# Two deformable convolutions: low halves to VectorE, tents and padded copies to ScalarE, images written out

## The reference

```python
x = x + deformable_conv(_ln_c(x))     # offsets from a 3x3 convolution, batch norm and relu
t = t + lstm_like(_ln_t(t))           # 256 steps, one after the other
x = x + deformable_conv(_ln_c(x))     # the second kind, without batch norm
t = t + top2_of_8_experts(_ln_t(t))
```

```python
py, px = base_y + ky - 1 + dy, base_x + kx - 1 + dx
sampled = (v00*(1-fy)*(1-fx) + v01*(1-fy)*fx + v10*fy*(1-fx) + v11*fy*fx) * mod
out = einsum('bckhw,ock->bohw', sampled, w)
```

## Time and profile before

| | us |
|---|---|
| median of 3 runs (1077.59 to 1084.23) | 1082.31 |
| the profiled execution | 1078.73 |
| its span, first to last instruction | 1076.9 |
| busy: TensorE | 802.8 |
| busy: VectorE | 648.6 |
| busy: ScalarE | 592.6 |
| busy: GpSimd | 439.1 |

### The profile page before, as it was taken

How to read it: one execution, slowest core, us unless ns; L and a number is a source line. 1 busy time by engine, 2 the same in 40 slices (tenths; PEclk the granted TensorE clock), 3 DMA queues, 4 the chain that set the end, 5 groups by cost and what they waited for, 6 DMA issues and landing times.

```text
span 1076.9 us, 18938 instructions
## 1 busy us (share of the span) xinstructions
PE 802.8 (75%) x6224; PEld 589.6 (55%) x6224; DVE 648.6 (60%) x1576; ACT 592.6 (55%) x1660; POOL 439.1 (41%) x343
## 2 busy tenths in 40 slices
PE   5687787666666666666666468886867999899996
PEld 3465575555555555555555435665653666556664
DVE  3999992355535445433333358999716776656775
ACT  1566664333335445333333336766646888778884
POOL 0577884000000000000000006878735888768885
PEclk9898988555555555555555568999876999999998
DMA  9500000000001100000000000000000010010000
GB/s 221 132 2 0 0 1 1 1 1 1 0 1 66 72 1 1 1 1 1 1 1 1 1 1 1 2 0 0 0 1 1 2 70 2 14 60 2 2 2 20
DMA packets 5852, 18.41 MB, mean 17 GB/s; under 512 B 1093, under 2 KB 2822, under 8 KB 5254
## 3 DMA queue, kind: packets, MB, share of 16 engines
q1 hardware_dynamic: 5478, 17.21, 5.6%
q10 hardware_dynamic: 288, 0.13, 0.1%
HBM read 9.47 MB, written 0.52 MB: 9 GB/s over the span
## 4 chain that ended last, share of the span: by engine, by line
POOL 35%; PE 20%; issue 19%; DVE 13%; ACT 11%; DVEq 1%; POOLq 1%; DMA 0%; SPq 0%; ACTq 0%
POOL zw L786 19%; POOL hid L750 15%; PE bank L463 9%; DVE bank L1036 6%; PE bank L465 5%; ACT scan_io L688 5%; ACT tcell L692 4%; DVE hr L1042 4%; PE bank L270 1%; PE bank L303 1%; POOL xs L743 1%; PE bank L282 1%; DVE st L875 1%; PE bank L275 1%; POOLq L785 1%
## 5 line engine op out<-in xcount | busy, mean ns | idle before, releaser
L750 POOL TENSOR_TENSOR hid<-smat,shi 128x512 f16<-128x512 f32 x144 | 216.4, 1526 | 556.1 <-ACT smat L594 555.9
L786 POOL TENSOR_TENSOR zw<-hid,zw 128x512 f16<-128x512 f32 x176 | 203.9, 1159 | 50.4 <-ACT zw L719 39.7
L463 PE MATMUL bank<-hr,lv 64*64 64x8 f32 x512 | 96.7, 261 | 158.1 <-DVE hr L1042 158.1
L463 PEld LDWEIGHTS bank<-hr,lv 64*64 64x64 f32 x512 | 72.5, 200 | 204.8 <-DVE hr L1042 204.7
L1141 DVE SCALAR_TENSOR_TENSOR hid<-bank,wsc,st 128x512 f32<-128x512 f32 x176 | 131.8, 750 | 77.0 <-ACT st L723 68.7
L688 ACT ACTIVATE scan_io<-bank 64x16 f32<-64x16 f32 x256 | 49.3, 193 | 210.7 <-PE bank L465 210.5
L1036 DVE TENSOR_TENSOR_SCAN bank<-scan_io 64x32 f32<-64x32 f32 x256 | 57.5, 224 | 162.3 <-ACT scan_io L688 162.2
L875 DVE TENSOR_TENSOR st<-tent,tentx 128x768 f32<-128x768 f32 x96 | 147.0, 1595 | 1.7
L503 PE MATMUL bank<-st,wh 128*128 128x512 f16 x352 | 136.7, 388 | 12.1 <-POOL st L779 5.4
L723 ACT ACTIVATE st<-bank,wsc 128x512 f32<-128x512 f32 x176 | 121.0, 687 | 35.5 <-PE bank L504 18.0
L504 PE MATMUL bank<-st,wl 128*128 128x512 f16 x352 | 136.6, 388 | 0.0
(11 more groups left out here) (149 smaller groups left out, 1275.2 us busy)
## 6 DMA issues: line engine op xcount, KB each, us to landing
w13s<-w SPq DMA_DIRECT2D x8, 704.0 KB, 16.4
w2f<-w SPq DMA_DIRECT2D x4, 384.0 KB, 26.9
w13s<-wh SPq DMA_DIRECT2D x2, 704.0 KB, 3.4
w13s<-wl SPq DMA_DIRECT2D x2, 704.0 KB, 4.6
wh<-w13s SPq DMA_DIRECT2D x2, 704.0 KB, 4.3
wl<-w13s SPq DMA_DIRECT2D x2, 704.0 KB, 5.4
w2f<-w2p SPq DMA_DIRECT2D x2, 384.0 KB, 5.2
w2p<-w2f SPq DMA_DIRECT2D x2, 384.0 KB, 6.2
```

The costliest lines, as they stand in the source:

```text
L463: nc.tensor.matmul(both[:, 0, t, :], lv[:, C:2 * C], prev, start=False, stop=True, skip_group_check=True)
L750: nc.gpsimd.tensor_tensor(slo[:, place(p, g), :, :], smat[:, g % RING, :, :], shi[:, place(p, g), :, :], ALU.subtract).then_inc(s(c + "s_l ...
L786: nc.gpsimd.tensor_tensor(hl[:, u % MR, :], hid[:, u % MR, :], hh[:, u % MR, :], ALU.subtract)\
```

## The change

It touches the two convolutions only.

- GpSimd keeps the residual addition alone. The low half comes from VectorE (`low`), which reads the transposed group from PSUM: scale, less the high half. `smat` and ScalarE's second copy are gone.
- TensorE may write a bank again only when VectorE's `low` of three groups before is done (`s_low`).
- ScalarE makes the tents (`far` is the absolute distance, then relu(1 - far)) and the padded copies.
- VectorE's work is spread over the groups: `low(m, g)` at each g, and between them outer products of this and the next image, `flats`, `distances`, `weighted`, `tap_images`.
- The steps of image m + 1 sit at other groups on TensorE and ScalarE. The loops are written out, and instructions that only counted semaphores up are gone.

```diff
 TensorE
-                    if waits(NG * m + g - RING + 2):
-                        pe.wait_ge(s(c + "tr_copied"), NG * m + g - RING + 2)
+                    if NG * m + g >= RING:
+                        pe.wait_ge(s(c + "s_low"), NG * m + g - RING + 1)
...
+                for m in range(B):
                     for g in range(NG):
+                        if m + 1 < B:
+                            if g < 2:
+                                offsets(m + 1, g)
+                            elif g == 3:
+                                turn_offsets(m + 1)
+                            elif g == 4:
+                                taps(m + 1, 0)
+                            elif g == 8:
+                                taps(m + 1, 1)
+                        if g == LAG + 2 and m > 0 and m % 2 == 0:
+                            turn(m // 2 - 1)
+                        turn_weights(m, g)
                         if g >= LAG:
+                            sums(m, g - LAG)
+                        elif m > 0:
+                            sums(m - 1, NG - LAG + g)
 ScalarE
+                def pads(m):
+                    if m > 1:
+                        act.wait_ge(s(c + "conv_done"), m - 1)
...
+                        nc.scalar.copy(dst[:, 1:1 + H, x0:x0 + W], src).then_inc(s(c + "pads"), 1)
+                def tents(m):
+                    act.wait_ge(s(c + "dist"), m + 1)
+                    nc.scalar.activation(far[:, :, :, :], dist[:, :, :, :], ACT.Abs).then_inc(s(c + "far"), 1)
+                    act.wait_ge(s(c + "far"), m + 1)
...
+                    nc.scalar.activation(tent[m % 2][:, :, :, :], far[:, :, :, :], ACT.Relu, scale=-1.0,
+                                         bias=epsc[:, 2:3]).then_inc(s(c + "tents"), 1)
+                def high(m, g):
+                    act.wait_ge(s(c + "tr_done"), NG * m + g + 1)
+                    if NG * m + g >= SR:
+                        act.wait_ge(s(c + "sz_done"), NG * m + g - SR + 1)
+                    nc.scalar.activation(shi[:, place(m % 2, g), :, :].rearrange("p k n -> p (k n)"),
                                          bank[3 + g % RING][:, :], ACT.Copy, scale=SSCALE)\
+                        .then_inc(s(c + "s_high"), 1)
...
+                            if g == 2:
+                                offsets(m + 1)
+                            elif g == 4:
+                                turned(m + 1)
+                            elif g == 5:
+                                tents(m + 1)
+                            elif g == 6:
+                                taps(m + 1, 0)
...
+                        if g == 7 and m + 2 < B:
+                            pads(m + 2)
+                        high(m, g)
+                    if m + 1 < B:
+                        taps(m + 1, 1)
 GpSimd
-                        gp.wait_ge(s(c + "tr_copied"), 1 + NG * m + g + 1)
-                        nc.gpsimd.tensor_tensor(slo[:, place(p, g), :, :], smat[:, g % RING, :, :],
-                                                shi[:, place(p, g), :, :], ALU.subtract).then_inc(s(c + "s_low"), 1)
 VectorE
+                def low(m, g):
+                    dve.wait_ge(s(c + "s_high"), NG * m + g + 1)
+                    nc.vector.scalar_tensor_tensor(out=slo[:, place(m % 2, g), :, :].rearrange("p k n -> p (k n)"),
+                                                   in0=bank[3 + g % RING][:, :], scalar=SSCALE,
+                                                   in1=shi[:, place(m % 2, g), :, :].rearrange("p k n -> p (k n)"),
+                                                   op0=ALU.mult, op1=ALU.subtract).then_inc(s(c + "s_low"), 1)
...
+                for m in range(B):
+                    for g in range(NG):
+                        low(m, g)
+                        if g == 0:
+                            outer(m, 2)
+                        elif 2 <= g <= 4:
+                            outer(m, g + 1)
+                        if g == 1 and m + 2 < B:
+                            flats(m + 2)
+                        if m + 1 < B:
+                            if g == 4:
+                                distances(m + 1)
+                            elif g == 5:
+                                weighted(m + 1)
+                            elif g == 6:
+                                outer(m + 1, 0)
+                                tap_images(m + 1, 0)
+                            elif g == 8:
+                                outer(m + 1, 1)
+                                tap_images(m + 1, 1)
```

More of the change, by code:

```diff
@@ L105, in build @@
         dist = sb("dist", [P, 2, 2 * TAPS, 16])
-        ndist = sb("ndist", [P, 2, 2 * TAPS, 16])
+        far = sb("far", [P, 2, 2 * TAPS, 16])
         tent = [sb(f"tent{p}", [P, 2, 2 * TAPS, 16]) for p in range(2)]
@@ L172, in place @@
             return (NG * p + g) % SR
-        def waits(v):
-            return not isinstance(v, int) or v > 0
         S = {}
@@ L185, in build @@
         for l in range(2):
-            for n in ("image", "taps", "conv_done", "om_sb", "omt_ps", "omt_sb", "z_ps", "z_act",
-                      "z_dve", "sig", "tent", "st_ready", "tr_done", "tr_copied", "s_low", "sz_done",
-                      "dist", "ndist", "tents", "osb", "out_ps", "out_sb", "res"):
+            for n in ("pads", "flat", "taps", "conv_done", "om_sb", "omt_ps", "omt_sb", "z_ps", "z_act",
+                      "z_dve", "sig", "tent", "st_ready", "tr_done", "s_high", "s_low", "sz_done",
+                      "dist", "far", "tents", "osb", "out_ps", "out_sb", "res"):
                 s(f"c{l}_{n}")
@@ L388, in conv @@
-                offsets(0, 0, 0)
-                offsets(0, 0, 1)
-                pe.wait_ge(s(c + "taps"), 2)
-                taps(0, 0, 0)
-                turn_offsets(0)
-                taps(0, 0, 1)
-                stream(0, 0, first=True)
-                with pe.Fori(0, BQ - 1) as i:
-                    stream(2 * i + 1, 1)
-                    stream(2 * i + 2, 0, ended=i)
-                stream(B - 1, 1, last=True)
+                offsets(0, 0)
+                offsets(0, 1)
+                turn_offsets(0)
@@ L480, in _ @@
             conv(1)
-            norm(3, [("c1_res", 1 + BQ)])
+            norm(3, [("c1_res", BQ)])
             for j in range(8):
@@ L634, in conv @@
-                offsets(0)
-                taps(0, 0, 0)
-                turned(0, 0)
-                taps(0, 0, 1)
-                stream(0, 0)
-                with act.Fori(0, BQ - 1) as i:
-                    stream(2 * i + 1, 1)
-                    stream(2 * i + 2, 0, ended=i)
-                stream(B - 1, 1, last=True)
+                act.wait_ge(s(f"n{2 * l}_xn"), 2)
+                pads(0)
+                pads(1)
+                offsets(0)
+                turned(0)
+                tents(0)
@@ L881, in conv @@
                 dve.wait_ge(s(f"n{2 * l}_xn"), 2)
-                dve.wait_ge(s("zero"), 2)
-                image(0, 0, 0)
+                flats(0)
                 split_taps(l)
-                image(1, 1, 0)
-                def batch(m, p, b4_next):
-                    offsets(m, p)
-                    outer(m, p)
-                    if b4_next is not None:
-                        image(m + 2, p, b4_next)
-                with dve.Fori(0, BQ - 1) as i:
-                    for p in range(2):
-                        batch(2 * i + p, p, i + 1)
@@ L895, in conv @@
-                for p in range(2):
-                    batch(B - 2 + p, p, None)
+                distances(0)
+                weighted(0)
+                outer(0, 0)
+                outer(0, 1)
+                tap_images(0, 0)
+                tap_images(0, 1)
+                flats(1)
+                for m in range(B):
+                    for g in range(NG):
[6 more added lines that the diff above has]
+                            flats(m + 2)
+                        if m + 1 < B:
+                            if g == 4:
[8 more added lines that the diff above has]
+                                tap_images(m + 1, 1)
```

220 lines of the change are left out of this document (92 added, 128 removed).

## The result

The changed kernel takes 1105.71 us (median of 4 runs, 1103.61 to 1106.83); the kernel before takes 1079.95 beside it (median of 4, 1077.59 to 1084.23). The ratio is 1.0232, 95% interval 1.0189 to 1.0274: slower by 25.8 us.

What follows compares the result with a forecast made beforehand. VectorE, busy 98% in the convolutions, was the bound; afterwards work 14.4, waits 4.15 and clock 1.5 give 20.1 us an image. 15.9 + 7 x 20.1 + 14.0 = 170.6 us per convolution, together +22.9: 1103 us, range 1074 to 1120.

Steps and rivals of the forecast that it cites:

- the work of VectorE: VectorE's instructions for one image in the convolutions after the change: 14.4 us, without waits.
- waits A: VectorE idle before low half 5, while ScalarE does far, tent and high half 5: 2.05 us per image.
- B: VectorE waits at group 8, as TensorE's taps, in front of transposes 8, need the low tap images: 1.25 us per image.
- C: VectorE waits before low half 1 of the next image, behind TensorE's transposes, sums and offsets: 0.75 us per image.
- the clock: TensorE's stop of some 5 us per image brings half clock on the work behind it: 1.5 us, bounds 0.8 to 1.7.
- the start-up: From the start of a convolution to its first low half: 15.9 us.
- The period: Time per image in the convolutions, work plus waits plus clock loss: 20.1 us, bounds 18.3 to 21.2.
- The last image: End of each convolution: nine low halves, four outer products, small waits and the unchanged tail: 14.0 us.
- The clock costs nothing: Rival, chance 0.24: TensorE's stop costs no clock in the convolutions; period 18.3 to 18.8 us, kernel 1081 us.
- VectorE stays the bound: Rival, chance 0.13: the waits shrink; with only the one before low half 5, period 16.5 us, kernel 1051 us.
- The clock never comes up: Rival, chance 0.03: TensorE at half clock throughout the convolutions; period 26 us, kernel 1184 us.
- The rule of the Trainium skill: Keep both tent steps on VectorE, not ScalarE: period about 0.85 us shorter, 12 us over both convolutions.

Runs made afterwards that it cites:

- e2: Changed kernel with ScalarE's tents and VectorE's weighted tents moved from group 5 to group 6: 1104.88 us.
- e5: Changed kernel with 64 unused matrix products on TensorE in front of the taps of group 8: 1084.49 us.
- e1: Changed kernel with the first half of the next image's taps and tap images one group earlier: 1070.45 us.
- e8: e3 with the first flat copy on ScalarE and VectorE's second flat moved to the next image: 1026.33 us.
- e3: Changed kernel reordered: taps one group earlier, tents one group later, distances one outer product earlier, outer(m + 1, 1) at group 7: 1025.72 us.
- e7: e3 with 144 GpSimd subtractions added on data nobody uses, one per high half: 1107.11 us.
- e4: Changed kernel with both tent instructions (absolute value and tent) back on VectorE, behind the distances: 1085.61 us.

## Why the prediction was right, point by point

The mechanism held: the work of VectorE, the waits A, B and C and the clock are where they were forecast, with about the sizes forecast. That the total fits to 3 us is in part luck, as two errors cancel (the start-up, and what lies outside the convolutions).

**VectorE's work.** 14.4 us an image were forecast, 14.35 measured (above); where an addition of GpSimd falls on an outer product it is 14.96 (from 90.36 on, 20.95 less waits of 5.99). The low half took 0.69 to its result and 0.60 to the next start, against 0.75 and 0.67 taken: cheaper by 0.6 an image. The flats and the weighted tents took that back, at 0.76 and 0.48 to the next start for 0.65 and 0.37, with the 0.08 of overlap that is lost at each of the four waits.

**Wait A.** Forecast 2.05, measured 2.04 in every image. That it fits to 0.01 is luck: the high half began 0.68 us after the tent where I had 0.57, and my 2.05 held 0.08 of lost overlap that the trace counts as VectorE's work and not as idle time. The other terms are as forecast: `far` starts 0.03 after the distances end (66.54 + 0.75 to 67.32) and takes 0.68. The place "in front of high half 5" that I named is not what counts, as e2 showed: it is a chain out to ScalarE and back with too little of VectorE's own work beside it.

**Waits B and C.** At full clock (e5) they are 1.30 and 0.88 for the forecast 1.25 and 0.75. e1 wrote the tap images earlier and 35 us went, more than wait B alone (14 x 1.3), as the stop and with it the clock changed too. So the mechanism that I called B, taps waiting for tap images in front of transposes 8, is shown.

**The clock.** Taken at 1.5 us an image, bounds 0.8 and 1.7. The changed kernel less e5 is 1105.7 - 1084.5 = 21.2 us over 14 periods, 1.5 each. The average is right, what it is made of only in part. I had 3.4 us at the lower level; in the image shown it is about 5, from 72.85 to 78.0, and costs 2.3 (0.89 on B, 1.41 on low half 0), above my bound of 1.7. Over the fourteen periods the difference to e5 goes from 2.6 down to 0.8. And it lands not on B and C but on B (2.19 for 1.30) and on low half 0 (1.56 for 0.15), behind the offset convolution's first half at 2.48 us. C did not change (0.89 against 0.88). The premise, that a stop of 3 to 4 us is followed by half the clock, is too plain. The stop in front of the slow stretch of the earlier trace rows was 4.28 us, and the same trace has one of 3.83 with the full level right behind it:

```profile
86.28 0.65 PE L336 MATMUL bank<-ident,st 128*128 128x128 f32 x4 [3.83 <-DVE st L875]
```

**The period** was 20.1 in the forecast. Seven of them lie between the first low half of image 0 (36.77) and that of image 7 (181.42): 144.65 / 7 = 20.66. In the second convolution the same two are

```profile
668.11 0.69 DVE L876 SCALAR_TENSOR_TENSOR hid<-bank,shi 128x512 f16<-128x512 f32 x1 [2.73 <-ACT shi L601]
...
809.40 0.68 DVE L876 SCALAR_TENSOR_TENSOR hid<-bank,shi 128x512 f16<-128x512 f32 x1
```

and 141.29 / 7 = 20.18.

**Mis-sized: the start-up.** The term "15.9" measured 36.77 - 17.59 = 19.2 in the first convolution and 668.11 - 649.72 = 18.4 in the second. I had summed taps, offsets, transposes and high half to 3.2 us at full clock. TensorE had stood 5.78 us for the first tap images, from 31.25 on it ran at the lower level, and these steps took 36.77 - 31.25 = 5.5. The first convolution has 0.8 more in front, as ScalarE's padded copies wait for VectorE's small instructions of the batch norm:

```profile
18.55 1.70 ACT L558 COPY pad<-xn 64x256 f32<-64x256 f32 x4 [4.54 <-DVE bnw L962]
```

The last image took 195.15 - 181.42 = 13.7, for 14.0. The first convolution is thus 19.2 + 144.7 + 13.7 = 177.6 against 170.6, the second 18.4 + 141.3 + 13.6 = 173.3. Of the 9.7 us by which both together exceed the forecast, 5.8 are the start-ups' and 4.5 the periods', less 0.6 for the last images.

**Not foreseen: 5.1 us outside the convolutions,** which hid half of that error in the total; there the forecast was lucky. The first matmuls of the norm behind each convolution (L265) take 1.98 us where they took 3.40 and 3.78. It may be that TensorE is no longer held up by GpSimd's nine last subtractions, 12.92 us, in front of them, but that is not shown. From L265 to the end of the span are 281.4 us, 283.7 before; from the first L265 to the second convolution 453.9, 455.4 before. In e8, which has no such subtractions, one of the two rows is back at 3.67, and the stretch behind it takes 283.1. That makes 1.5 and 2.3 us. The remaining 1.2 lie in front of the first convolution and are not the change's: its normalised input comes at 16.90 here and at 18.12 before, and over all eleven traces at 16.5 to 18.3 whatever the edit (18.16 in e1, 16.73 in e3, 18.25 in e7).

**The rivals.** "The clock costs nothing" was forecast at 1081 and is, in effect, e5: 1084.5. "VectorE stays the bound" would have been faster, and is what e3 reaches, by an order that the change doesn't have: 14.8 us a period against the 14.4 + 2.05 that I gave it. "The clock never comes up" found no support, and e3 and e5 run at 1.00 with all 36 transposes of an image. The Trainium skill's sentence on transposes (TensorE: Matmul & The Clock Gate, section Part 4: PE-mode transpose) would have the clock stay down under them. In e3, where transposes fill 23.4 of the 60 us from 40 to 100, the granted clock is 1.00; the profile lists them as MATMUL and doesn't show whether they run in the mode that the sentence is about.

**The rule of the Trainium skill** that spoke against the tents on ScalarE (ScalarE: Activation LUTs, section Rules for kernel authors) was worth 12 us in the prediction and 20 in e4, of which about 8 go with the clock. The rule is right here. Its reason, the speed of one element, which it gives for bf16, is the smaller part: in float32 `tent` takes 0.46 on VectorE and 0.78 on ScalarE, but `far` takes 0.76 and 0.68, 1.22 us against 1.46 together. The larger part is the way to ScalarE and back, 2.04 us of waiting. And in e3, where the chain is covered, ScalarE's tents stand on no one's path.

## What to carry to other kernels

When work moves to an engine that feeds the one it came from, count the round trip: two hand-overs and three instructions of ScalarE cost VectorE 2.04 us here for 1.2 us of work saved, until one outer product of its own and a group's distance covered them. Before judging such a change by its time, look at which instruction stands in front of each wait in every queue; the same instructions ran in 1106 us in one order and in 1026 in another. And look at stops of TensorE even where it is not the bound, and fill them, if what it does right behind the stop is what others wait for.

## What the runs showed of the hardware

The length of a stop of TensorE alone doesn't tell the level behind it. Behind the fourteen stops of 1.15 to 1.50 us in e5 the tap matmuls took 0.65. Behind those of 4.7 to 5.1 in the changed kernel they took 1.07 to 1.12, but 0.80 behind one of 4.88. In between both occur: 0.65 and 1.12 behind 2.44 and behind 3.12 (e1), behind 3.43 and behind 4.11 (e4).

64 matrix products without use (3.74 us of TensorE an image) made the kernel 21 us faster, and 40 made e1 14 us faster.

A subtraction of GpSimd beside VectorE slows the outer product from 0.95 us to as much as 2.02, and leaves the low half, which has one operand in PSUM, at 0.67 to 0.69.
